# The final addition of the last stage is done by POOL instead of VectorE

## The reference

```python
    x = x + _L0_gnn_ref(_layernorm(x, axis=-1), edge_index, ...)
    x = x + _L0_ffn_ref(_layernorm(x, axis=-1)[None], ...)[0]
```

```python
        h = jax.nn.relu(jnp.einsum('bsd,bfd->bsf', x, W1m) + b1m[:, None, :])
        out = jnp.einsum('bsf,bdf->bsd', h, W2m) + b2m[:, None, :]
        res = x + out
        mu = res.mean(axis=-1, keepdims=True)
        var = res.var(axis=-1, keepdims=True)
        return (res - mu) * jax.lax.rsqrt(var + LN_EPS) * lng + lnb
```

## Time and profile before

| | us |
|---|---|
| median of 3 timed runs | 3344.33 (3344.17 to 3345.43) |
| the profiled execution, its own time | 3327.99 |
| its span, first to last instruction | 3326.3 |
| busy in the span: PE / DVE / ACT / POOL | 2743.9 / 2818.5 / 1689.0 / 844.1 |
| mean granted TensorE clock | 0.916 of full speed |
| the last stage, about | 2880 to 3326 |

### The profile page before, as it was taken

How to read it: one execution, slowest core, us unless ns; L and a number is a source line. 1 busy time by engine, 2 the same in 40 slices (tenths; PEclk the granted TensorE clock), 3 DMA queues, 4 the chain that set the end, 5 groups by cost and what they waited for, 6 DMA issues and landing times. The chain is left out here.

```text
span 3326.3 us, 41230 instructions
## 1 busy us (share of the span) xinstructions
PE 2743.9 (82%) x11205; PEld 1838.8 (55%) x11205; DVE 2818.5 (85%) x5994; ACT 1689.0 (51%) x4291; POOL 844.1 (25%) x741
## 2 busy tenths in 40 slices
PE   7999997777777199999977777771899999688886
PEld 5777774333333078888843333330688888555554
DVE  7999996999999566767759999995988887399999
ACT  4545552555555433333315555553778787144443
POOL 0022212333332033333333333321333332000000
PEclk8999998889888589999988898885899999899998
DMA  9989997444443288887754444433999997388886
GB/s 322 344 300 318 319 335 268 133 153 150 152 154 121 72 271 274 271 266 261 251 198 142 150 152 155 149 105 131 379 357 351 350 345 269 129 292 287 293 291 226
DMA packets 332178, 788.76 MB, mean 237 GB/s; under 512 B 55070, under 2 KB 55616, under 8 KB 321738
## 3 DMA queue, kind: packets, MB, share of 16 engines
q1 hardware_dynamic: 265464, 622.14, 53.7%
q0 software_dynamic: 64032, 160.18, 15.1%
q10 hardware_dynamic: 2452, 3.79, 0.3%
HBM read 510.62 MB, written 329.28 MB: 253 GB/s over the span
## 5 line engine op out<-in xcount | busy, mean ns | idle before, releaser
L862 PE MATMUL bank<-wr,nT_e 128*128 128x512 f32 x1280 | 690.0, 689 | 241.7 <-ACT nT_e L662 241.4
L862 PEld LDWEIGHTS bank<-wr,nT_e 128*128 128x128 f32 x1280 | 268.5, 221 | 561.2 <-issue 292.3
L1019 PE MATMUL bank<-whi,t_hi 128*128 128x512 f32 x1256 | 525.1, 418 | 24.3 <-DVE t_lo L405 24.3
L1021 PE MATMUL bank<-whi,t_lo 128*128 128x512 f32 x1256 | 499.3, 398 | 0.0
L1020 PE MATMUL bank<-wlo,t_hi 128*128 128x512 f32 x1256 | 499.1, 397 | 0.0
L640 POOL DMA_INDIRECT nv_e<-rows,dst_row x160 | 255.6, 1598 | 701.8 <-ACT w_e L680 563.7
L677 ACT ACTIVATE w_e<-vs_e,ex_e 128x128 f32<-128x128 f32 x640 | 204.3, 390 | 336.3 <-DVE acc_e L794 251.6
L1019 PEld LDWEIGHTS bank<-whi,t_hi 128*128 128x128 f32 x1256 | 238.0, 189 | 74.6 <-issue 17.8
L1021 PEld LDWEIGHTS bank<-whi,t_lo 128*128 128x128 f32 x1256 | 238.1, 190 | 59.0
L1020 PEld LDWEIGHTS bank<-wlo,t_hi 128*128 128x128 f32 x1256 | 238.5, 190 | 45.1
L1209 PE MATMUL bank<-g_hi,whi 128*128 128x512 f32 (+1 forms) x640 | 263.0, 411 | 0.0
(11 more groups left out here) (244 smaller groups left out, 5852.9 us busy)
## 6 DMA issues: line engine op xcount, KB each, us to landing
rows<-t_row SPq DMA_DIRECT2D x312, 512.0 KB, 3.9
touched<-done_e SPq DMA_DIRECT2D x160, 256.0 KB, 2.0
xin<-in_x SPq DMA_DIRECT2D x156, 256.0 KB, 4.7
xTin<-in_xT SPq DMA_DIRECT2D x156, 256.0 KB, 3.5
vin<-rows SPq DMA_DIRECT2D x156, 256.0 KB, 4.0
g_vin<-rows SPq DMA_DIRECT2D x156, 256.0 KB, 5.7
g_xin<-in_x SPq DMA_DIRECT2D x156, 256.0 KB, 6.4
x_table<-g_shifted SPq DMA_DIRECT2D x156, 256.0 KB, 6.2
```

Source lines behind the costliest of these rows:

```text
L862: pe.matmul(psR[b][:, :], nT[:, b, cc, :], wr[:, cc, :], start=(cc == 0), stop=False)
L1019: pe.matmul(ps, hi[:, cc, :], whi[:, cc, :], start=(cc == 0), stop=False)
L1021: last = pe.matmul(ps, lo[:, cc, :], whi[:, cc, :], start=False, stop=(cc == KC - 1))
```

## The change

The step `final` leaves DVE's list and becomes the only step of a list on POOL, with the same operands, the same two waits and the same semaphore raised at its end. Nothing else differs.

```diff
+        @block.gpsimd
+        def _(pool):
+            def final(t):
+                r, u = size(t), t % FY
+                pool.wait_ge(s["scaled"], t + 1)
+                pool.wait_ge(s["loaded"][t % FX], 16 * (t // FX + 1))
+                pool.tensor_tensor(y[0:r, u, :], y[0:r, u, :], x1[0:r, t % FX, :], ALU.add).then_inc(s["final"], 1)
+
+            pipeline(n_tiles, [(final, 0)])
+
         @block.vector
         def _(dve):
...
-            def final(t):
-                r, u = size(t), t % FY
-                dve.wait_ge(s["scaled"], t + 1)
-                dve.wait_ge(s["loaded"][t % FX], 16 * (t // FX + 1))
-                dve.tensor_tensor(y[0:r, u, :], y[0:r, u, :], x1[0:r, t % FX, :], ALU.add).then_inc(s["final"], 1)
-
-            pipeline(n_tiles, [(scale, 2), (measure, 6), (invert, 4), (final, 2), (low_units, 10)])
+            pipeline(n_tiles, [(scale, 2), (measure, 6), (invert, 4), (low_units, 10)])
```

## The result

The changed kernel took 3292.49 us (median of 4 runs, 3290.27 to 3292.98), the kernel before 3344.88 us in the same comparison: 52.4 us less, a ratio of 0.9842 (95% interval 0.9825 to 0.9859). The forecast was 3306.

The account below looks back on a forecast made before the run. DVE's path was taken to bound the last stage; 0.61 us per tile saved less 0.37 us held by POOL leaves 0.24, times 157 tiles 38 us, off the 3344.33 us median: 3306 us, 8-in-10 range 3262 to 3332.

Parts of the forecast that it names:

- What bounds the stage: Last stage: DVE is the only engine without gaps, its path taking 10.85 us per group of four tiles.
- What leaves DVE: Last stage: 157 additions leave DVE's path, each giving back its spacing of 0.61 us, 96 us if nothing replaced them.
- The wait that is not in the code: DVE's offset L1408 and the scaling wait until POOL's SBUF-reading addition is done, taken as a full wait.
- Its size: Offset L1408 starts at 1.96 instead of 1.59 us, 0.37 late, so a tile gives back 0.24 us.
- A: DVE and POOL don't disturb each other in the last stage: 3267 us with DMA bound at 353 GB/s, else 3248; chance 0.2.
- B: Only DVE's wide scaling is held, the one-column offset slips through: 61 us gained, 3283 us; chance 0.1.
- C: POOL's addition costs its upper bound, 1.67 us, so each tile loses 0.23 us: slower, 3380 us; chance 0.13.
- D: The two effects cancel, POOL's addition taking 1.40 to 1.48 us with hand-over: within 7 us of before; chance 0.04.

Follow-up runs that it names:

- Experiment 1: Changed kernel, but POOL writes one column of a scratch tile in place of the addition, behind the same waits; 3249.41 us, ratio 0.972.
- experiment 2: Changed kernel, but POOL fills 1460 columns of a scratch tile, reading nothing, in place of the addition; 3250.93 us, ratio 0.9725.
- experiment 3: Changed kernel, but POOL adds only columns 0 to 255 of the 512; 3248.87 us, ratio 0.9723.
- experiment 4: Changed kernel, but DVE's offset takes one tensor input and the reciprocal as a per-partition scalar; 3272.97 us, ratio 0.979.
- experiment 5: Changed kernel, but ACT writes the centred rows to PSUM, where DVE's scaling reads them, with a sixth bank; 3292.77 us, ratio 0.9844.
- experiment 9: Changed kernel, but POOL copies the scaled rows to a scratch tile instead of adding x1; 3247.68 us, ratio 0.9717.
- experiment 12: Changed kernel with one-input offset, scaling reading PSUM (sixth bank), and low units 9 tiles ahead instead of 10; 3252.38 us, ratio 0.9731.
- experiment 6: Changed kernel with both the one-input offset and the scaling reading the centred rows from PSUM (sixth bank); 3287.73 us, ratio 0.9838.

## Why the prediction was right, and by how much not

*What bounds the stage.* Right: DVE's path, tile by tile. Experiment 1 found the floor at 3249 us where the prediction had 3248 without a bound by DMA.

*What leaves DVE.* Right: 0.61 us a tile. Experiment 1 took 94 us of the 96 off the median of its own comparison (3343.5 to 3249.4).

*The wait that is not in the code.* Right in place and kind: the offset L1408 (now L1418) is held, and with it the scaling. I had taken the full wait as the cautious end with no row for it; experiments 1 to 5 show it. The Trainium skill's rule (SBUF - State Buffer, Who interferes with whom) says that a DVE instruction with two SBUF inputs contends with a GpSimd instruction that reads SBUF and not with one that only writes it. The traces agree: held by the addition (0.45 instead of 0.16 us), by the constant addition (0.60) and by the copy (0.58), not by the write of experiment 2 (0.159). By the same rule the later instruction is blocked until the other is done. Here it was blocked for 1.12 us of the addition's 1.27 and for 0.47 of the constant addition's 1.49, and the measurement decides.

*Its size: the term that was off.* I had the addition end at 1.92 and the offset start at 1.96, 0.37 late, so 0.24 us gained a tile. Measured: POOL starts at 0.76 instead of 0.72 (the hand-over cost 0.08, not 0.04), is recorded for 1.27 instead of 1.20, but holds DVE only for its first 1.12 us. So the offset goes on at 1.88 and the next scaling starts at 0.76 + 1.12 + 0.08 = 1.96, 0.32 us earlier than before. The 0.04 that I added for DVE to go on after the hold was not there. The recorded duration was too low by 0.07 and was also the wrong length to use; the two errors partly cancelled. That 1.20 came so near 1.27 is luck as well: I had it from the copy, at 1.09 us for 512 columns, and a copy of 512 columns took 0.613 (experiment 9), so the pace of the 79 columns was wrong and the second input costs far more than the 0.11 that I added for it.

*One tile in four was not looked at.* I took every tile as a plain one of 2.28 us. The timeline of before, of the tile behind the low units:

```profile
3101.14 0.69 DVE L1413 TENSOR_TENSOR f_y<-f_y,ln_g 128x512 f32<-128x512 f32 x1
...
3101.87 0.70 DVE L1398 BATCH_NORM_STATS2 f_st<-bank 128x6 f32<-128x512 f32 x1
...
3103.55 0.69 DVE L1413 TENSOR_TENSOR f_y<-f_y,ln_g 128x512 f32<-128x512 f32 x1
```

It took 3103.55 - 3101.14 = 2.41 us, for its statistics start 0.73 us after the scaling, not 0.60. After, it took 1.97 (3100.99 to 3102.96 above), a gain of 0.44, as POOL's addition sets the length of either kind of tile. So a group gains 3 x 0.32 + 0.44 = 1.40 us instead of 4 x 0.24 = 0.96, and 39 groups make 55 us instead of 38. From the first low units to the last it was 52.0 us (2890.7 to 3305.9 before, 2906.7 to 3269.9 after), and the start and the end of the stage, which I had costed at nothing within 1 us, took 1.5 us more: 50.5; the medians differ by 52.4.

*The rivals.* A (no disturbance) falls with the 0.424 us of the offset, and its bound of 353 GB/s was no bound: 374 GB/s went through in experiment 1. What one stage carries need not be what another can. B falls with experiment 5. C needed hand-over and addition together over 1.48 us; they took 0.08 and 1.27. D had no part; as it was worked out, an addition of 1.40 with the hand-over in it would still gain 157 x 0.08 = 13 us, not stay within 7.

## What to carry to other kernels

An elementwise instruction that is moved from DVE to POOL gives back its spacing on DVE, less the time for which it stands in the way of DVE's next instruction with two SBUF inputs, however narrow that is; look there in the recorded durations, not in the list of waits. That time need not be POOL's recorded duration (1.12 of 1.27 us, 0.47 of 1.49), and an overlap that costs nothing may only have missed it: before calling a pair free, look for a place where the two start together. If such an instruction can be rewritten with a per-partition scalar or with one input in PSUM, the whole gain is to be had, here 90 us instead of 52. But check what the rewritten instruction frees: a bank that is freed one step later gave back most of it until one look-ahead was changed.

## What the runs showed of the hardware that was not expected

- POOL's addition of 128 x 512 took 1.266 us, of 384 columns 0.997, of 256 columns 0.724: 2.1 ns a column and some 0.18 us.
- It holds a two-input DVE instruction from its start for 1.11 to 1.14 us at 512 columns, about 0.14 us less than its recorded duration, and for 0.84 us at 384 columns and 0.57 at 256. Even an offset over one column waits: near the end of the stage one lasted 1.25 us.
- On POOL a constant addition with one input took 1.49 us, more than the two-input one; a copy took 0.61 us. The estimate from 79 columns (1.09 us) fits neither. Both hold a two-input DVE instruction for their first 0.47 us alone. Why the constant addition is so slow, and why it holds for less than a third of its time, stays open.
- The hold works the other way too: in experiment 4 an addition of POOL's that started 0.16 us behind a scaling with two SBUF inputs took 1.64 us instead of 1.27; in experiment 12, with the scaling's input in PSUM, one that started as closely took 1.26.
- A DVE offset with a per-partition scalar took 0.21 us, against 0.16 with two tensor inputs, and is not held, not even when it starts 0.02 us behind the addition (0.21 in experiments 4, 6 and 12).
- The stage's DMA share was 1.02 at 374 GB/s, and no engine is said to wait for a DMA from 2920 to 3230 us (experiments 1 to 3); the loads of x1 landed after 7.3 us in the changed kernel, against 5.2, which the look-ahead covers.
